# Norms of the first batch and weight magnitudes moved into the last unit of the first attention

## The chip, the cores and the metric

The kernel runs on one core of one Trainium2 chip. The metric is the device time of one execution in microseconds (us). The core has five engines that work side by side, each through its own queue and in its own order: TensorE (PE in the profile, with its weight loads as PEld), VectorE (DVE), ScalarE (ACT), GpSimd (POOL) and SyncE (SP, which issues DMAs). They wait for one another by semaphores.

## The reference, cut to what matters

Four layers follow one another on x, of shape (2, 1024, 256): an attention with 16 heads, a feed-forward with ternary weights, a small attention with 32 heads, and a gated feed-forward. The change touches the seam between the first two.

```python
x = x + layernorm(attention_0(layernorm(x)))
x = x + layernorm(ffn_0(layernorm(x)))
...
def ffn_0(x):                       # w1, w2: (704, 256), w3: (256, 704)
    q = lambda w: clip(round(w / (mean(abs(w)) + 1e-8)), -1, 1)
    return (sigmoid(x @ q(w1).T) * (x @ q(w2).T)) @ q(w3).T
```

So between attention_0 and ffn_0 there are two layer norms (of the attention's result y, and then of the new x) and three sums of |w|, one for each weight.

## The kernel before, in words

x and y live on chip as 16 tiles of 128 tokens by 256 features; tiles 0 to 7 are the first batch, 8 to 15 the second.

`attention_0` runs 32 units u = 2h + b, one for each of the 16 heads h and the two batches b. A unit has eight steps p, one for each tile of queries, in the order of sizes 8, 1, 7, 2, 6, 3, 5, 4 blocks of 128 keys. For each step there is a chain: PE scores, DVE maximum (L801), ACT exponent (L673), PE transposes (L524), ACT high half (`turned_hi`, L668), DVE low half (`turned_lo`, L796), PE context (L539). The engines' orders are written out by hand in `unit`: at step p PE turns step p+1 and scores step p+3, ACT copies the turned step p+1 and takes the exponent of p+3, DVE makes the low half of p+1 and the maximum of p+3. After step 3 and step 7 ACT and DVE split the context (L679, L805), and PE multiplies it by the output weights (`out`, L504), whose result DVE adds to y (`add_out`, L787). The last two add_out of a unit are done at p = 1 of the next unit. So y of the first batch is final after the add_out calls at p = 1 of the last unit (u = 31, a unit of the second batch), and y of the second batch is final with the last instructions of the attention. In the last unit nothing of a next unit is to be projected, and POOL (which rotates queries and keys) has nothing left to do.

Then comes a barrier of all engines (`end_phase`) and `normed_ffn`. Its ramp: ACT sums the magnitudes of the three weights (L949, one Abs over 1536 columns each), DVE takes statistics of y's tiles (L142), the variance (L152 to L157), ACT the square root (L163), DVE the normaliser (L169 to L175); ACT scales four tiles of y and POOL adds them to x (L1241); then POOL scales (L1252) and adds the others. The same norm steps follow for x's first four tiles, ACT scales these (`scale_x`, L1101), PE turns them (L1044), ACT and DVE split them (L1108, L1181). The first half of the ternary weights is made on DVE by `weights.vector(0)` (L959 to L968) after a small matmul of the totals (L954), the second half by `weights.vector(1)`, the third matrix by `weights.vector(2)`.

The body has 4 chunks of 512 tokens (ch), each with 6 hidden tiles (ht), s = 6 ch + ht. For each s: PE `gate_up` (L1057, 8 matmuls of 512 columns), ACT `sigmoid` (L1114), DVE `product` (L1196), ACT `hidden_high` (L1121), DVE `hidden_low` (L1201). PE may begin s only when product s-2 is done. At ht = 0 the variance of the next chunk's x, at ht = 1 its normaliser and scale_x, at ht = 4 of chunk 0 its turning; `down` (L1072) of a chunk runs at ht = 1 of the next. The square root, the exponential and the sigmoid need different tables on ACT, so each change between them is an ACT_TABLE_LOAD in the trace. Copy, Identity and Abs run with any of these tables.

Of the kernel before, what the change touches and what calls it, by code (L numbers as in the profile page):

```python
# [124 lines left out]
class Moments:  # L125
# [22 lines left out]
    def variance(self, dve, g):  # L148
        t0, t1 = self.groups[g]
        dve.wait_ge(self.stats_ready, t1)  # L150
# [120 lines left out]
def program(nc, ins, out):  # L271
    with ExitStack() as ctx:
        c = Core(nc, ctx)
        constants(c, ins["L0_attn_hidden_states"])
        with ExitStack() as wctx:
            raw = RawWeights(c, "f0", F0, [ins[f"L0_ffn_w{j}"] for j in (1, 2, 3)], wctx)
            attention_0(c, ins, lambda loads: norm_and_turn(c, "in", LoadPadded(c, raw, loads)), raw)
            c.end_phase()
            normed_ffn(c, "f0", Ternary(c, raw, wctx), WSCALE, 1.0, True)
# [19 lines left out]
def attention_0(c, ins, before, raw):  # L299
# [22 lines left out]
    with ExitStack() as ctx:  # L322
# [87 lines left out]
        with nc.Block() as block:  # L410
# [28 lines left out]
            def _(pool):  # L439
# [197 lines left out]
            def _(act):  # L637
# [43 lines left out]
                def unit(h, b):  # L681
                    u = 2 * h + b
                    for p in range(TB):
# [33 lines left out]
                        if p == 7 and exists(u + 2):  # L717
                            rope_hi(u + 2, b, 0)

# [29 lines left out]
                units(act, unit)  # L749

            @block.vector
            def _(dve):
# [56 lines left out]
                def unit(h, b):  # L809
                    u = 2 * h + b  # L810
                    for p in range(TB):
# [35 lines left out]
                        if p == 7:  # L847
                            add_out(u, h, b, 1)

# [22 lines left out]
                add_out(NU - 1, H0 - 1, 1, 3)  # L872

# [54 lines left out]

class Ternary:
# [4 lines left out]
    def __init__(self, c, raw, ctx):  # L934
        self.c, self.raw = c, raw
        self.total = c.psum[:, 4, 0:3]
        self.scrap = c.sb("scrap", [P, raw.cols], F32, ctx)
        self.mag, self.gam, self.pos, self.neg = (c.sb(f"q_{n}", [P, 3], F32, ctx) for n in ("mag", "gam", "pos", "neg"))
# [3 lines left out]
        self.mag_ready, self.total_ready, self.thr, self.below_ready, self.ready = (  # L942
            c.sem(n) for n in ("mag_ready", "total_ready", "thr", "below_ready", "q_ready"))

    def scalar(self, act, j):
        if j == 0:
            act.wait_ge(self.raw.loaded, self.raw.landed)
        wait(act, self.mag_ready, j)
        act.activation(self.scrap[:, :], self.raw.buf[:, j, :], ACT.Abs,  # L949
                       accum_out=self.mag[:, j:j + 1]).then_inc(self.mag_ready, 1)  # L950

    def tensor(self, pe):
        pe.wait_ge(self.mag_ready, 3)
# [45 lines left out]
def normed_ffn(c, name, weights, y_unit, unscale, sigmoid_only, out=None):  # L999
# [12 lines left out]
    by_chunk = [(TPC * ch, TPC * ch + TPC) for ch in range(CHUNKS)]  # L1012

    with ExitStack() as ctx:
# [6 lines left out]
        y_norm = Moments(c, f"{name}_y", [(0, NT // 2), (NT // 2, NT)], ctx, y_unit)  # L1021
        x_norm = Moments(c, f"{name}_x", by_chunk, ctx)
# [12 lines left out]
        with c.nc.Block() as block:  # L1035
# [54 lines left out]
            def _(act):  # L1090
# [6 lines left out]
                def scale_x(ch):  # L1097
                    act.wait_ge(x_norm.norm_ready, 2 * ch + 2)
                    wait(act, turned, 2 * (ch - 1))
                    for t in range(TPC * ch, TPC * ch + TPC):  # L1100
                        act.activation(xn[:, ch % 2, t % TPC:t % TPC + 1, :], c.x[:, t:t + 1, :], ACT.Identity,  # L1101
                                       bias=x_norm.shift[:, t:t + 1], scale=x_norm.rstd[:, t:t + 1]).then_inc(xn_ready, 1)
# [20 lines left out]
                def result(ch):  # L1123
                    act.wait_ge(x_added, TPC * ch + TPC)
# [11 lines left out]
                x_norm.root(act, 0)  # L1136
                scale_x(0)
                y_norm.root(act, 1)
                high(0)
                for ch in range(CHUNKS):  # L1140
                    for ht in range(HT):
                        s = ch * HT + ht
                        sigmoid(s)
                        if s >= 1:
                            hidden_high(s - 1)
                        if ht == 0 and ch + 1 < CHUNKS:
                            x_norm.root(act, ch + 1)
# [18 lines left out]
            def _(dve):  # L1166
                def x_variance(ch):
                    dve.wait_ge(x_added, TPC * ch + TPC)
                    x_norm.statistics(dve, c.x, TPC * ch, TPC * ch + TPC)
                    x_norm.variance(dve, ch)  # L1170
# [33 lines left out]
                y_norm.statistics(dve, c.y, 0, NT // 2)  # L1204
                y_norm.variance(dve, 0)
                y_norm.normaliser(dve, 0)
                y_norm.statistics(dve, c.y, NT // 2, NT)
                x_variance(0)
                x_norm.normaliser(dve, 0)
                y_norm.variance(dve, 1)  # L1210
                weights.vector(dve, 0)
                low(0)
                y_norm.normaliser(dve, 1)
                weights.vector(dve, 1)
                for ch in range(CHUNKS):
                    for ht in range(HT):
                        s = ch * HT + ht
                        product(s)
                        if s >= 1:
                            hidden_low(s - 1)  # L1220
                        if ht == 0 and ch + 1 < CHUNKS:
                            x_variance(ch + 1)
                        if ht == 1 and ch + 1 < CHUNKS:
                            x_norm.normaliser(dve, ch + 1)
# [14 lines left out]
            def _(pool):  # L1239
# [6 lines left out]
                for t in range(TPC):  # L1246
                    pool.wait_ge(y_normed, t + 1)
                    add_y(t)
                for t in range(TPC, NT):
                    if t == NT // 2:  # L1250
                        pool.wait_ge(y_norm.norm_ready, 4)
                    pool.tensor_scalar(c.y[:, t:t + 1, :], c.y[:, t:t + 1, :], y_norm.rstd[:, t:t + 1], y_norm.shift[:, t:t + 1],  # L1252
                                       ALU.mult, ALU.add).then_inc(y_scaled, 1)
                    pool.wait_ge(y_scaled, t - TPC + 1)
# [578 lines left out]
```

## Time and profile before

| | us |
|---|---|
| median of 3 runs | 1802.39 (1800.43 to 1804.83) |
| the profiled execution, whole time | 1805.49 |
| its span, first to last instruction | 1803.7 |
| first attention, up to the barrier | about 937.6 |
| ramp of the first feed-forward, to its first gate matmul | 937.6 to 957.2 |
| its chunk 0, to the first matmul of chunk 1 | 957.2 to 981.1 |

Over the span PE is busy 90%, DVE 76%, ACT 61%, POOL 38%; the mean granted TensorE clock is 0.961. These shares are averages over all four layers. The slices around the middle of the span (each 45 us) show PE falling from 9 tenths to 5 and 6 at the seam, with DVE still at 7 and 8. The profiled execution is 3.1 us longer than the median.

The rows further down come from two views. In the busy time by stretch, a row gives the stretch (us from the start of the span), its length, the busy us and number of instructions of PE, PEld, DVE, ACT and POOL, the granted TensorE clock (1.00 is the full 2.4 GHz, 0.50 is 1.2 GHz), and the DMA share and GB/s. In the timeline, a row gives start, duration, engine, line, operation, output <- inputs, shapes, count, and in brackets the idle time before it and what ended it.

### The profile page before, as it was taken

What the parts mean: (1) busy time and instruction counts of PE and PEld (TensorE: products, weight loads), DVE (VectorE), ACT (ScalarE), POOL (GpSimd) and SP (SyncE); (2) the same over time, 40 slices, a digit from 0 to 9 for tenths busy, and PEclk for the clock granted to TensorE, in tenths of its full rate; (3) what the DMA queues carried; (4) which work ended last, traced back from release to release, by engine and by line L of the source; (5) the groups of instructions that cost most, each with busy time, mean ns of one, the idle gap of its engine ahead of it and who ended that gap; (6) DMA issues with size and microseconds to landing.
All of it is one profiled execution on the core that took longest, in us unless ns stands there. A gap on an engine that the chain in (4) does not pass through costs nothing. (4 is left out here: it accounts for less than half of the span.)

```text
span 1803.7 us, 42731 instructions
## 1 busy us (share of the span) xinstructions
PE 1622.6 (90%) x14612; PEld 1012.8 (56%) x14612; DVE 1364.0 (76%) x2792; ACT 1091.7 (61%) x2092; POOL 691.3 (38%) x804
## 2 busy tenths in 40 slices
PE   3899999999999999999956838899999999985997
PEld 1577777777777777777743534233333333333555
DVE  3477877877887887887767657988888888936674
ACT  4566666666666666666645652356566666665553
POOL 1655555555555555555503235021212222224012
PEclk9899999999999999999987969999999999987999
DMA  4322111121121121121100030000000010000001
GB/s 137 93 51 49 46 43 47 44 55 44 44 47 44 44 55 44 44 53 38 35 1 0 1 109 12 16 16 13 17 13 17 12 18 11 10 1 1 1 13 36
DMA packets 53108, 61.85 MB, mean 34 GB/s; under 512 B 11345, under 2 KB 32018, under 8 KB 53010
## 3 DMA queue, kind: packets, MB, share of 16 engines
q1 hardware_dynamic: 53010, 60.55, 13.8%
q8 instruction: 61, 1.00, 0.2%
q14 instruction: 37, 0.30, 0.1%
HBM read 18.57 MB, written 2.10 MB: 11 GB/s over the span
## 5 line engine op out<-in xcount | busy, mean ns | idle before, releaser
L1634 ACT ACTIVATE a_prob<-psum 128x1024 f32<-128x1024 f32 (+3 forms) x384 | 290.8, 812 | 188.8 <-PE psum L1598 188.8
L1674 DVE TENSOR_REDUCE a_mx<-psum 128x1 f32<-128x512 f32 (+3 forms) x608 | 369.2, 656 | 41.3 <-PE psum L1580 28.3
L1666 POOL TENSOR_SCALAR_AFFINE_SELECT a_prob<-a_prob 128x256 f32<-128x256 f32 x256 | 103.0, 408 | 386.8 <-ACT a_prob L1634 384.2
L1577 PE MATMUL psum<-a_kd,a_qp 128*128 128x512 f16 (+3 forms) x768 | 223.0, 337 | 17.8 <-DVE a_mx L1674 6.8
L445 POOL TENSOR_TENSOR a_swp<-a_swp,a_sin 128x512 f32<-128x512 f32 x128 | 163.4, 1276 | 161.6 <-DMA a_swp<-a_lin 130.8
L801 DVE TENSOR_REDUCE a_nmax<-psum 128x1 f32<-128x1024 f32 (+7 forms) x256 | 191.3, 748 | 0.6 <-PE psum L516 0.6
L673 ACT ACTIVATE a_prob_big<-psum,a_nmax 128x1024 f32<-128x1024 f32 (+3 forms) x128 | 122.0, 953 | 102.9 <-DVE a_nmax L801 101.2
L1577 PEld LDWEIGHTS psum<-a_kd,a_qp 128*128 128x128 f16 x768 | 70.6, 98 | 188.1 <-DVE a_mx L1674 139.0
L449 POOL TENSOR_TENSOR a_rope<-a_swp,a_cosd 128x512 f32<-128x512 f32 x128 | 164.2, 1282 | 12.5 <-POOL a_swp L445 4.8
L1619 PE MATMUL psum<-a_prob,a_vg 128*32 128x512 f32 (+3 forms) x1536 | 164.5, 500 | 1.9 <-POOL a_prob L1666 1.4
L796 DVE TENSOR_TENSOR a_pt_lo_big<-psum,a_pt_hi_big 128x512 f16<-128x512 f32 (+3 forms) x256 | 138.5, 582 | 30.2 <-ACT a_pt_hi_big L668 30.2
L539 PE MATMUL psum<-a_pt_hi_big,a_v_hi 128*128 128x128 f16 x832 | 146.0, 219 | 1.3 <-issue 1.0
L539 PE MATMUL psum<-a_pt_hi_big,a_v_lo 128*128 128x128 f16 x832 | 146.0, 219 | 0.0
L539 PE MATMUL psum<-a_pt_lo_big,a_v_hi 128*128 128x128 f16 x832 | 145.9, 219 | 0.0
L455 POOL TENSOR_TENSOR a_q_lo<-a_rope,a_q_hi 128x512 f16<-128x512 f32 x64 | 78.3, 1225 | 141.4 <-ACT a_q_hi L650 141.4
L771 DVE SCALAR_TENSOR_TENSOR a_cosd<-psum,a_head_bias,a_cos 128x512 f32<-128x512 f32 x128 | 95.8, 749 | 40.7 <-ACT a_lin L643 34.6
L643 ACT ACTIVATE a_lin<-psum,a_head_bias 128x512 f32<-128x512 f32 x128 | 88.7, 693 | 61.6 <-PE psum L482 59.9
L515 PE MATMUL psum<-a_k_hi,a_q_hi 128*128 128x512 f16 (+3 forms) x384 | 125.7, 327 | 0.0
L515 PE MATMUL psum<-a_k_lo,a_q_hi 128*128 128x512 f16 (+3 forms) x384 | 125.3, 326 | 0.0
L515 PE MATMUL psum<-a_k_hi,a_q_lo 128*128 128x512 f16 (+3 forms) x384 | 123.7, 326 | 0.0
L524 PE MATMUL psum<-ident,a_prob_big 128*128 128x128 f32 x832 | 116.4, 276 | 4.8 <-ACT y L745 3.5
L668 ACT ACTIVATE a_pt_hi_big<-psum 128x512 f16<-128x512 f32 (+3 forms) x256 | 118.5, 522 | 1.6 <-PE psum L524 1.5
(278 smaller groups left out, 4391.6 us busy)
## 6 DMA issues: line engine op xcount, KB each, us to landing
a_swp<-a_lin SPq DMA_DIRECT2D x256, 128.0 KB, 2.3
a_qp<-a_q_part SPq DMA_DIRECT2D x192, 16.0 KB
a_kd<-a_k_part SPq DMA_DIRECT2D x192, 16.0 KB
x<-_attn_hidden_states_dram SPq DMA_DIRECT2D x4, 512.0 KB, 5.6
a_w_raw<-in_L_attn_Wq_dram SPq DMA_DIRECT2D x16, 128.0 KB, 2.3
a_w_raw<-in_L_attn_Wk_dram SPq DMA_DIRECT2D x16, 128.0 KB, 2.3
a_w_raw<-in_L_attn_Wv_dram SPq DMA_DIRECT2D x16, 128.0 KB, 2.3
a_wo_raw<-in_L_attn_Wo_dram SPq DMA_DIRECT2D x1, 2048.0 KB
```

What stands on the lines that cost most here:

```text
L445: pool.tensor_tensor(swp[:, ch, :], swp[:, ch, :], sin[:, (i % 2) * BANK:(i % 2 + 1) * BANK], ALU.mult).then_inc(sin_done, 1)
L449: pool.tensor_tensor(rope[:, ch, :], swp[:, ch, :], cosd[:, ch, :], ALU.add).then_inc(rope_ready, 1)
L515: last = pe.matmul(scores(p, a, e), qq[:, b, rows], kk[:, b, a:e], start=(m == 0), stop=(m == 2 and e < n))
L539: last = pe.matmul(dst, vv[:, b, j, :], pp[p % 2][:, (p // 2) % 2, cols], start=(j == 0 and m == 0), stop=(j == BLOCKS[p] - 1 and m == 2))
L668: act.activation(pt_hi[p % 2][:, (p // 2) % 2, j0 * P:j1 * P], c.psum[:, turned_bank(at), 0:(j1 - j0) * P], ACT.Copy).then_inc(pt_hi_done, 1)
L673: act.activation(prob[p % 2][:, (p // 2) % 2, 0:BLOCKS[p] * P], scores_row(p), ACT.Exp, bias=nmax[:, b, p:p + 1], accum_out=rowsum[:, b, p ...
L796: dve.tensor_tensor(pt_lo[p % 2][:, (p // 2) % 2, cols], c.psum[:, turned_bank(at), 0:(j1 - j0) * P], pt_hi[p % 2][:, (p // 2) % 2, cols], ...
L801: dve.tensor_reduce(nmax[:, b, p:p + 1], scores_row(p), AX.X, ALU.max, negate=True).then_inc(max_done, 1)
L1577: last = pe.matmul(to[:, j * n:(j + 1) * n], qp[:, w % 3, t * P:(t + 1) * P], kd[:, w % 3, j0 + j, a:e], start=True, stop=not edge)
L1619: last = pe.matmul(c.psum[j * R:(j + 1) * R, 4, a % BANK:a % BANK + e - a], vg[:, u % 2, kt, :], prob_at(u, 2 * n)[:, j, a % BANK:a % BANK ...
L1634: act.activation(prob_at(u, i)[:, 2 * pair:2 * pair + 2, a % BANK:a % BANK + e - a], c.psum[:, pair_of(u, i):pair_of(u, i) + 2, 0:e - a], ...
L1674: dve.tensor_reduce(mx[:, t, j0:j0 + per, a // BANK], work(("S", w, i))[:, 0:per * (e - a)].rearrange("p (j n) -> p j n", j=per), AX.X, AL ...
```

## The change

The norm of y's first batch, its addition to x, the norm of x's first four tiles and the three magnitudes are issued inside the last unit of the attention by a new helper `FirstBatch`; what is left of the norms of the second batch goes into chunk 0 of the feed-forward.

```diff
 (attention_0: GpSimd, after its loop)
+                lead.gpsimd(pool)
 (attention_0: ACT, at the end of each step p of a unit)
+                        if not exists(u + 1):
+                            lead.scalar(act, p, wo_raw[:, 0:raw.cols // D, :].rearrange("p h d -> p (h d)"))
 (ACT, after the units)
+                lead.scalar_last(act)
 (attention_0: DVE, at the end of each step p)
+                        if not exists(u + 1):
+                            if p == 1:
+                                dve.wait_ge(y_done, 4 * u)
+                            lead.vector(dve, p)
 (DVE, after the last add_out)
+                lead.vector_last(dve)
...
+class FirstBatch:
+    def vector(self, dve, p):
+        if p == 1:
+            self.y_norm.statistics(dve, self.c.y, 0, TB)
+            self.y_norm.variance(dve, 0)
+        if p == 3:
+            self.y_norm.normaliser(dve, 0)
+    def vector_last(self, dve):
+        dve.wait_ge(self.x_added, TPC)
+        self.x_norm.statistics(dve, self.c.x, 0, TPC)
+        self.x_norm.variance(dve, 0)
+        self.x_norm.normaliser(dve, 0)
+    def scalar(self, act, p, scrap):
+        if p == 2:
+            self.y_norm.root(act, 0)
+        if p in (4, 5, 6):
+            j = p - 4
+            if j == 0:
+                act.wait_ge(self.raw.loaded, self.raw.landed)
+            wait(act, self.mag_ready, j)
+            act.activation(scrap, self.raw.buf[:, j, :], ACT.Abs, accum_out=self.mag[:, j:j + 1]).then_inc(self.mag_ready, 1)
+    def scalar_last(self, act):
+        self.x_norm.root(act, 0)
+        act.wait_ge(self.mag_ready, 3)
+    def gpsimd(self, pool):
+        y, x = self.c.y, self.c.x
+        pool.wait_ge(self.y_norm.norm_ready, 2)
+        for t in range(TB):
+            pool.tensor_scalar(y[:, t:t + 1, :], y[:, t:t + 1, :], self.y_norm.rstd[:, t:t + 1], self.y_norm.shift[:, t:t + 1],
+                               ALU.mult, ALU.add).then_inc(self.y_scaled, 1)
+            pool.wait_ge(self.y_scaled, t + 1)
+            pool.tensor_tensor(x[:, t:t + 1, :], x[:, t:t + 1, :], y[:, t:t + 1, :], ALU.add).then_inc(self.x_added, 1)
+        pool.wait_ge(self.x_added, TB)
...
 (Ternary: no Abs any more, and PE's wait for the magnitudes goes)
     def tensor(self, pe):
-        pe.wait_ge(self.mag_ready, 3)
...
 (normed_ffn: ACT)
                 weights.scalar(act, 0)
-                y_norm.root(act, 0)
-                scale_y()
+                if not lead:
+                    y_norm.root(act, 0)
+                    scale_y()
...
+                        if lead and ch == 0 and ht == 2:
+                            y_norm.root(act, 0)
 (normed_ffn: DVE)
+                if lead:
+                    weights.vector(dve, 0)
+                    low(0)
+                else:
...
                 weights.vector(dve, 1)
                 for ch in range(CHUNKS):
                     for ht in range(HT):
                         s = ch * HT + ht
                         product(s)
                         if s >= 1:
                             hidden_low(s - 1)
+                        if lead and ch == 0 and ht == 1:
+                            y_norm.statistics(dve, c.y, NT // 2, NT)
+                            y_norm.variance(dve, 0)
+                        if lead and ch == 0 and ht == 3:
+                            y_norm.normaliser(dve, 0)
```

In the first feed-forward `y_norm` now covers the second batch alone and `x_norm` chunks 1 to 3, and POOL begins with tile 8. The Abs results that nobody reads go into the raw output weights, which are no longer needed, in place of a buffer of their own. The second feed-forward is built without the helper and is as before.

## Rows read from the trace of the kernel before

**Rows 1.** Busy time by stretch: last unit, ramp, chunk 0.
```profile
907.00:937.60 30.60, 21.54 (x227) 17.38 (x227) 19.03 (x42) 11.92 (x29) 0.00 (x0) 0.93 0.00 1
937.60:957.16 19.56, 2.69 (x10) 1.93 (x10) 17.18 (x60) 13.04 (x21) 7.92 (x12) 0.50 0.00 1
957.16:981.10 23.94, 17.38 (x56) 6.79 (x57) 18.52 (x40) 11.88 (x20) 12.22 (x16) 0.71 0.00 1
```

**Rows 2.** Timeline, last unit: start, duration, engine, line, [idle before, releaser].
```profile
918.78 0.58 ACT L673 ACTIVATE a_prob_small<-psum,a_nmax 128x384 f32<-128x384 f32 x1 [1.10 <-DVE a_nmax L801]
...
919.35 0.86 ACT L668 ACTIVATE a_pt_hi_big<-psum 128x512 f16<-128x512 f32 x2
...
921.76 0.79 ACT L673 ACTIVATE a_prob_big<-psum,a_nmax 128x640 f32<-128x640 f32 x1 [0.79 <-DVE a_nmax L801]
...
923.06 0.56 DVE L796 TENSOR_TENSOR a_pt_lo_small<-psum,a_pt_hi_small 128x384 f16<-128x384 f32 x1 [0.65 <-ACT a_pt_hi_small L668]
...
924.93 0.76 ACT L668 ACTIVATE a_pt_hi_big<-psum 128x512 f16<-128x512 f32 x2
...
927.05 0.60 ACT L668 ACTIVATE a_pt_hi_small<-psum 128x512 f16<-128x512 f32 x1 [1.37 <-PE psum L524]
...
930.75 0.60 ACT L679 ACTIVATE a_ctx_hi<-psum 128x512 f16<-128x512 f32 x1 [3.10 <-PE psum L539]
...
935.23 0.88 DVE L787 SCALAR_TENSOR_TENSOR y<-psum,a_rsum,y 128x256 f32<-128x256 f32 x2 [0.41 <-PE psum L504]
```

**Rows 3.** Timeline, the ramp of the first feed-forward.
```profile
937.64 1.48 ACT L949 ACTIVATE scrap<-f_raw 128x1536 f32<-128x1536 f32 x1 [6.29 <-PEq L81]
937.66 2.71 DVE L142 BATCH_NORM_STATS2 f_y_stats<-y 128x6 f32<-128x256 f32 x8 [1.56 <-PEq L81]
...
939.23 1.28 ACT L163 ACT_TABLE_LOAD   x1
...
941.25 0.21 ACT L163 ACTIVATE f_y_sd<-f_y_var 128x8 f32<-128x8 f32 x1 [0.74 <-DVE f_y_var L157]
941.57 0.20 DVE L169 RECIPROCAL f_y_inv<-f_y_sd 128x8 f32<-128x8 f32 x1 [0.35 <-ACT f_y_sd L163]
...
942.56 0.16 DVE L175 TENSOR_SCALAR f_y_rstd<-f_y_half 128x8 f32<-128x8 f32 x1
...
947.96 0.59 PE L954 MATMUL psum<-q_mag,ones 128*128 128x3 f32 x2 [12.77 <-ACT scrap L949]
...
951.06 2.08 ACT L1101 ACTIVATE f_xn<-x,f_x_shift,f_x_rstd 128x256 f32<-128x256 f32 x4 [1.34 <-DVE f_x_rstd L175]
...
952.65 0.62 DVE L965 TENSOR_SCALAR below<-f_raw,q_neg 128x768 f16<-128x768 f32 x1
...
957.17 0.61 PE L1057 MATMUL psum<-xT_hi,ternary 128*128 128x512 f16 x1 [2.86 <-DVE xT_lo L1181]
```

**Rows 4.** Timeline, chunk 0.
```profile
959.82 1.08 DVE L965 TENSOR_SCALAR below<-f_raw,q_neg 128x768 f16<-128x768 f32 x1
...
962.05 0.68 DVE L1196 TENSOR_TENSOR f_hid<-psum,f_sig 128x512 f32<-128x512 f32 x1
...
967.23 0.60 ACT L1114 ACTIVATE f_sig<-psum 128x512 f32<-128x512 f32 x1
...
968.69 0.58 PE L1057 MATMUL psum<-xT_hi,ternary 128*128 128x512 f16 x1 [4.00 <-DVE f_hid L1196]
...
973.54 0.58 ACT L1114 ACTIVATE f_sig<-psum 128x512 f32<-128x512 f32 x1
...
978.57 0.68 DVE L1196 TENSOR_TENSOR f_hid<-psum,f_sig 128x512 f32<-128x512 f32 x1
...
981.10 0.39 PE L1057 MATMUL psum<-xT_hi,ternary 128*128 128x512 f16 x1 [0.73 <-DVE xT_lo L1181]
```

**Rows 5.** Stretches of the L1057 matmuls alone: s = 3, and s = 6.
```profile
968.60:973.00 4.40, 3.57 (x8) 1.02 (x8) 0.50 0.00 0
981.05:982.80 1.75, 1.70 (x8) 0.79 (x9) 1.00 0.00 0
```

More of the change, by code:

```diff
@@ L296, in spans, with attention_0 @@
         lo = end
-def attention_0(c, ins, before, raw):
+def attention_0(c, ins, before, raw, lead):
     nc = c.nc
@@ L926, in gpsimd_first, with __init__ @@
             pool.memset(buf[:, :, raw.width:raw.tiles * P] if j < 2 else buf[:, raw.width // P, :], 0.0).then_inc(self.padded, 1)
+class FirstBatch:
+    TILES = TB
+    def __init__(self, c, raw, ctx):
+        self.c, self.raw = c, raw
+        self.y_norm = Moments(c, "lead_y", [(0, TB)], ctx, WSCALE)
+        self.x_norm = Moments(c, "lead_x", [(0, TPC)], ctx)
+        self.mag = c.sb("q_mag", [P, 3], F32, ctx)
+        self.y_scaled, self.x_added, self.mag_ready = (c.sem(n) for n in ("lead_y_scaled", "lead_x_added", "lead_mag_ready"))
+    def vector(self, dve, p):
[30 more added lines that the diff above has]
+        pool.wait_ge(self.x_added, TB)
@@ L941, in __init__, with scalar @@
         self.parts = [[raw.view(self.ternary, j)] for j in range(3)]
[L942 to L950, printed above, removed]
+        self.total_ready, self.thr, self.below_ready, self.ready = (
+            c.sem(n) for n in ("total_ready", "thr", "below_ready", "q_ready"))
+    def scalar(self, act, piece):
+        pass
     def tensor(self, pe):
-        pe.wait_ge(self.mag_ready, 3)
         pe.matmul(self.total, self.c.ones[:, :], self.mag[:, :], start=True, stop=True).then_inc(self.total_ready, 1)
@@ L996, in vector, with normed_ffn @@
                                      in1=self.parts[j][0][:, :, cols], op0=ALU.mult, op1=ALU.subtract).then_inc(self.ready, 1)
-def normed_ffn(c, name, weights, y_unit, unscale, sigmoid_only, out=None):
+def normed_ffn(c, name, weights, y_unit, unscale, sigmoid_only, out=None, lead=None):
     HT = weights.raw.tiles
@@ L1101, in scale_x @@
                         act.activation(xn[:, ch % 2, t % TPC:t % TPC + 1, :], c.x[:, t:t + 1, :], ACT.Identity,
-                                       bias=x_norm.shift[:, t:t + 1], scale=x_norm.rstd[:, t:t + 1]).then_inc(xn_ready, 1)
+                                       bias=norm.shift[:, t:t + 1], scale=norm.rstd[:, t:t + 1]).then_inc(xn_ready, 1)
                 def high(ch):
@@ L1123, in result @@
                 def result(ch):
-                    act.wait_ge(x_added, TPC * ch + TPC)
+                    wait(act, x_added, TPC * ch + TPC - DONE)
                     for i in range(2):
@@ L1167, in x_variance @@
                 def x_variance(ch):
-                    dve.wait_ge(x_added, TPC * ch + TPC)
+                    wait(dve, x_added, TPC * ch + TPC - DONE)
                     x_norm.statistics(dve, c.x, TPC * ch, TPC * ch + TPC)
-                    x_norm.variance(dve, ch)
+                    x_norm.variance(dve, ch - X0)
                 def e_variance(ch):
@@ L1202, in hidden_low @@
                                       ALU.subtract).then_inc(hid_lo, 1)
[L1204 to L1213, printed above, removed]
+                if lead:
+                    weights.vector(dve, 0)
+                    low(0)
+                else:
+                    y_norm.statistics(dve, c.y, 0, NT // 2)
+                    y_norm.variance(dve, 0)
+                    y_norm.normaliser(dve, 0)
+                    y_norm.statistics(dve, c.y, NT // 2, NT)
+                    x_variance(0)
+                    x_norm.normaliser(dve, 0)
+                    y_norm.variance(dve, 1)
+                    weights.vector(dve, 0)
+                    low(0)
+                    y_norm.normaliser(dve, 1)
                 weights.vector(dve, 1)
@@ L1220, in _ @@
                             hidden_low(s - 1)
+                        if lead and ch == 0 and ht == 1:
+                            y_norm.statistics(dve, c.y, NT // 2, NT)
+                            y_norm.variance(dve, 0)
+                        if lead and ch == 0 and ht == 3:
+                            y_norm.normaliser(dve, 0)
                         if ht == 0 and ch + 1 < CHUNKS:
```

48 lines of the change are left out of this document (28 added, 20 removed).

## The prediction

> **What bounds the kernel at the seam.** I read the busy time by stretch first, then the timeline of each engine from 907 to 990 us, then the waits. The stretches [rows 1] show three pieces. The ramp, from the barrier to the first gate matmul, is 19.56 us with PE busy for 2.69 of them: this is the time the change is after. The last unit of the attention is not full either: in 30.6 us PE is busy 21.54, DVE 19.03, ACT 11.92 and POOL 0. It looks as if there were room for everything. The timeline says otherwise [rows 2]. Each exponent waits for DVE's maximum (idle 1.10 and 0.79), each low half on DVE waits for ACT's high half (0.65), and the high half at 919.35 and the one at 924.93 start right behind an exponent with no idle at all. So in this unit ACT and DVE take turns on one chain: maximum, exponent, turning, high half, low half, the next maximum. Their idle time is the other's turn. What is put into either queue on its turn lengthens the chain one for one; what is put where that engine waits anyway is free up to the length of that wait.
>
> **What goes into the last unit, in order of steps p.**
> - p = 1, DVE: eight statistics and the variance, from 937.66 to the root at 941.25 [rows 3], so 3.6 us, ahead of the maximum for which the exponent at 918.78 waits. On the chain: +3.6.
> - p = 2, ACT: the root, a table load of 1.28 and a root of 0.21 with gaps [rows 3], between the exponent at 918.78 and the high half at 919.35, which had no idle before it [rows 2]: +1.6.
> - The exponent table has to be loaded again before the exponent at 921.76. That one idles 0.79 [rows 2], and the 1.28 fits but for 0.5; ACT gets there a little earlier after the root, since PE will have caught up: bounds 0.3 and 0.5, taken +0.4.
> - p = 3, DVE: the normaliser, 941.57 to 942.72, 1.15 [rows 3]. DVE idles 0.65 there, plus the 0.4 just gained: +0.1.
> - p = 4, ACT: the first Abs, 1.6 from its start at 937.64 to the next start at 939.23 [rows 3], ahead of the high half at 924.93 that had no idle [rows 2]: +1.6.
> - p = 5, ACT: the second Abs, ahead of the high half at 927.05 that idles 1.37 [rows 2]: +0.2.
> - p = 6, ACT: the third, ahead of the context copy that idles 3.10 [rows 2]: 0.
> - POOL's eight tiles begin after the normaliser; at 12.22 us for 16 instructions [rows 1] a tile (two instructions) is 1.5 us, four are ready 6 us later, all eight 12 us later, and the unit has some 15 us to go. Covered. The new wait on y_done at p = 1 is for DVE's own previous instructions: nothing.
>
> Sum of the last unit: 3.6 + 1.6 + 0.4 + 0.1 + 1.6 + 0.2 = +7.5.
>
> **Behind the last add_out** (935.23 plus 0.88 [rows 2]) DVE alone does x's norm: half of the eight statistics, 1.35, then variance, root and normaliser as in rows 3; 942.72 - 937.66 - 1.35 = 3.7. The square root's table load hides in ACT's wait. The barrier follows at the same distance as before. +3.7.
>
> **The ramp.** Once y's norm, x's norm and the magnitudes are gone, two chains start with the block. ACT's scale_x at 951.06 led to the gate matmul at 957.17, 6.1 us [rows 3]; that is the upper end, since half of it was a wait for DVE. DVE's thresholds: the matmul of the totals, 0.59, three small operations of 0.16 with their waits, about 0.5, then 957.17 - 952.65 = 4.5 [rows 3]. Together 5.65, taken. The ramp was 957.17 - 937.64 = 19.5, so -13.9. PE's removed wait costs nothing on its own, it is in this sum.
>
> **Chunk 0, counted from its first gate matmul.** Before, product 0 came at 4.9, held by the second half of the ternary weights on a DVE that POOL was slowing (the same operation takes 0.62 at 952.65 and 1.08 at 959.82 [rows 3, 4], POOL working beside the second). Now POOL is idle there and PE's eight matmuls at the lower clock, 3.5 us [rows 5], come last: -1.35. From product 0 to sigmoid 1 it was 5.2 (962.05 to 967.23 [rows 4]), now product 0.6, statistics and variance 2.2, root and table load 1.55: -0.8. So sigmoid 1 is 2.15 earlier. Then DVE takes the second batch's eight statistics and variance ahead of the normaliser that scale_x(1) and sigmoid 2, behind it on ACT, wait for: +3.55, less 0.3 for the now undisturbed normaliser; balance +1.1. At ht = 2 ACT loads the root's table, takes the root and loads the sigmoid's again ahead of the sigmoid that stood at 973.54: 2.9 by rows 3; DVE had 0.4 us of its own there, so the chain is at +3.6. At ht = 3 DVE has the normaliser, +1.15, and then the third weight matrix beside POOL, which has just been released: by the 0.62 and 1.08 above, between 0 and +1.4 for its first operation and little for its second, taken +0.9. The product at 978.57 and with it the low half that PE waits for at 981.10 [rows 4] come 5.7 later relative to the first gate.
>
> **The clock.** PE idled 4.00 us before 968.69, and the following eight matmuls took 3.57 us at a granted clock of 0.50 (1.2 GHz); at 981.10 it had idled 0.73 and they took 1.70 at 1.00 (2.4 GHz) [rows 4, 5]. With chunk 0 stretched, PE will idle some 5 us before chunk 1, and its first eight matmuls stand on the path: +1.8. In the last unit PE will idle about 4 us before the last turning; the context and output matmuls behind it are on the path. Bounds 0 (clock stays) and +2.6 (all that follows at half); taken +1.2.
>
> **The sum.** 7.5 + 3.7 - 13.9 + 5.7 + 1.8 + 1.2 = +6.0 us. From chunk 1 on nothing is changed but POOL's tiles, which end before the next norm, so the shift is carried to the end. On its own execution 1805.5 becomes 1811.5; on the median 1802.4 becomes 1808.4.
>
> **A rule against the change.** In the trace a table load costs 1.28 us and the next activation starts at once (939.23; in the ramp it even runs ahead of the wait for the variance [rows 3]).
> The Trainium skill, ScalarE: Activation LUTs, What ACT_TABLE_LOAD costs, adds a drain of about 1.38 us to every switch. By that rule four added switches on the path would cost 5.5 us more and the time would be 1813.9; the trace does not show such a drain, so it has a small chance here.
>
> **The rivals.**
> - The idle shares are real room: what is inserted in the last unit hides. Then only the tail, ramp and chunk 0 count: 3.7 - 13.9 + 5.7 + 1.8 = -2.7, no measurable change; and if the second batch's statistics, root and normaliser in chunk 0 hide as well (-5.7 - 1.8), -10.2, that is 1792.2. For it: PE runs up to three steps ahead. Against: the four brackets in rows 2 and the high halves that start without idle. It turns faster once more than 9.6 of the 15 us on both chains hide. Chance 0.13, spread from 1792 to 1798.
> - The steps are as told but the clock does not fall in either place and the contention is nil: 6.0 - 1.8 - 1.2 - 0.9 = +2.1, 1804.5, within the noise. Chance 0.3 for this and for a partial hiding.
> - The clock falls in the last unit and stays low through the tail: +2.6 in place of 1.2, with the full 1.4 of contention: +7.9, 1810.3. Chance 0.14. With the drain on top, 1813.9 or more: 0.03.
> - POOL's additions come late and DVE waits for x_added ahead of the barrier. The cover is 9 us (four tiles ready 6 us after the normaliser, 15 to go); only if a tile took 3.7 us, against 1.5, would it show. 0.02, and +1 or +2.
>
> **How the numbers follow.** The forecast as summed, between 1806 and 1810, has 0.38. A measurement of this kernel can tell about 0.2%, 3.6 us, from no change: faster means under 1798.8, slower over 1806.0. From the cases: faster 0.13, same 0.30, slower 0.57. The range leaves out most of the fast case and the drain: 1800.5 to 1812.5.
>
> **What would show it.** In the profile of the changed kernel: the barrier about 11 to 13 us later than 937.6; gate 0 5.6 us after it, about 954 to 956; the exponent of step 5 waiting for the maximum behind the statistics; two more table loads in the last unit and two more in chunk 0; sigmoid 3 preceded by one; the first matmul of chunk 1 between 984 and 987 at a clock of 0.50 after an idle of 4 us or more. The forecast is wrong if the barrier comes less than 8 us later (room in the last unit), or if the first matmul of chunk 1 comes before 981 (room in chunk 0).

## The result, and the profile after

The changed kernel takes 1808.57 us (median of 20 runs, 1803.78 to 1810.96) against 1802.05 (median of 20, 1800.43 to 1804.83). The ratio of the runs is 1.0031, 95% interval 1.0024 to 1.0037: slower by 5.6 us (4.3 to 6.7). The forecast was 1808.4, +6.0. The profiled execution took 1808.71, its span is 1807.0.

The busy time by stretch of the kernel after: last unit with its tail and the barrier, ramp, chunk 0. Columns as in [rows 1].

```profile
905.00:947.90 42.90, 25.81 (x227) 20.16 (x227) 26.27 (x78) 20.47 (x40) 10.14 (x16) 0.79 0.00 1
947.90:953.50 5.60, 2.66 (x10) 1.93 (x10) 4.82 (x10) 4.55 (x7) 0.00 (x0) 0.50 0.00 0
953.50:982.20 28.70, 15.75 (x56) 6.27 (x56) 20.04 (x54) 14.55 (x23) 5.08 (x4) 0.74 0.00 1
```

The ramp went from 19.56 to 5.6 us, as meant. The last unit and chunk 0 grew by more than that: 30.6 to 42.9 (with the tail in it) and 23.9 to 28.7.

The last unit in the timeline of the kernel after, DVE and ACT, with PE's last turning; it answers to [rows 2]. L675 is the exponent, L670 the high half, L973 the Abs.

```profile
914.34 1.65 DVE L792 SCALAR_TENSOR_TENSOR y<-psum,a_rsum,y 128x256 f32<-128x256 f32 x4
916.03 2.71 DVE L142 BATCH_NORM_STATS2 lead_y_stats<-y 128x6 f32<-128x256 f32 x8
...
920.41 0.58 ACT L675 ACTIVATE a_prob_small<-psum,a_nmax 128x384 f32<-128x384 f32 x1 [4.68 <-DVE a_nmax L806]
...
921.10 1.28 ACT L163 ACT_TABLE_LOAD   x1
...
922.51 0.85 ACT L670 ACTIVATE a_pt_hi_big<-psum 128x512 f16<-128x512 f32 x2
...
923.87 1.28 ACT L675 ACT_TABLE_LOAD   x1
925.16 0.79 ACT L675 ACTIVATE a_prob_big<-psum,a_nmax 128x640 f32<-128x640 f32 x1
...
928.33 1.47 ACT L973 ACTIVATE a_wo_raw<-f_raw 128x1536 f32<-128x1536 f32 x1
...
929.80 0.75 ACT L670 ACTIVATE a_pt_hi_big<-psum 128x512 f16<-128x512 f32 x2
...
931.25 1.09 PE L526 MATMUL psum<-ident,a_prob_small 128*128 128x128 f32 x4 [3.35 <-DVE a_pt_lo_big L801]
...
932.38 0.60 ACT L670 ACTIVATE a_pt_hi_small<-psum 128x512 f16<-128x512 f32 x1 [0.36 <-PE psum L526]
...
937.44 0.60 ACT L681 ACTIVATE a_ctx_hi<-psum 128x512 f16<-128x512 f32 x1 [3.00 <-PE psum L541]
...
941.90 0.88 DVE L792 SCALAR_TENSOR_TENSOR y<-psum,a_rsum,y 128x256 f32<-128x256 f32 x2 [0.41 <-PE psum L506]
```

Ahead of the statistics nothing was changed, and the group of four add_out operations in front of them is the point from which both traces are counted (916.30 in the kernel before, 914.34 here; in the fourteen profiles of this study it lies between 912.95 and 916.30, so the first 900 us alone differ by up to 3 us from one execution to another, and spans are compared less well than steps). What to see: the exponent of step 5 waits 4.68 us where it waited 1.10, then come a table load, the root, another table load, and at 928.33 an Abs where the high half used to stand. The last turning takes 1.09 in place of 0.63.

The ramp and chunk 0 of the kernel after, answering to [rows 3, 4]:

```profile
942.69 1.40 DVE L142 BATCH_NORM_STATS2 lead_x_stats<-x 128x6 f32<-128x256 f32 x4
...
953.52 0.61 PE L1114 MATMUL psum<-xT_hi,ternary 128*128 128x512 f16 x1 [2.35 <-DVE xT_lo L1245]
...
963.43 2.70 DVE L142 BATCH_NORM_STATS2 f_y_stats<-y 128x6 f32<-128x256 f32 x8
...
971.08 1.28 ACT L163 ACT_TABLE_LOAD   x1
972.37 0.21 ACT L163 ACTIVATE f_y_sd<-f_y_var 128x8 f32<-128x8 f32 x1
972.60 1.28 ACT L1173 ACT_TABLE_LOAD   x1
973.89 0.60 ACT L1173 ACTIVATE f_sig<-psum 128x512 f32<-128x512 f32 x1
...
977.80 2.00 DVE L1023 SCALAR_TENSOR_TENSOR ternary<-f_raw,q_pos,below 128x1536 f16<-128x1536 f32 x1
...
978.28 2.10 POOL L1314 TENSOR_TENSOR x<-x,y 128x256 f32<-128x256 f32 x1
...
982.25 0.61 PE L1114 MATMUL psum<-xT_hi,ternary 128*128 128x512 f16 x1 [4.93 <-DVE xT_lo L1245]
...
985.94 0.69 DVE L1260 TENSOR_TENSOR f_hid<-psum,f_sig 128x512 f32<-128x512 f32 x1 [2.55 <-PE psum L1114]
...
989.14 0.71 DVE L155 TENSOR_SCALAR f_x_m<-f_x_m 128x4 f32<-128x4 f32 x1
```

The same five marks read in every profiled execution of the study, in us. Unit: from the four add_out operations at step 1 of the last unit to the end of the last add_out. Seam: from there to the first gate matmul. Chunk 0: from there to product 6 (the first of chunk 1). Variance: product 6 to product 7. The sum is that of the four. These columns are read from one execution of each kernel, and the ratio from all its runs. The profiled executions of e5, e10 and e12 took 1803.73, 1795.62 and 1803.24 us, 4 to 5 us less than the medians of their kernels, that of e4 took 4 us more (1808.06): so the sums and the ratios need not agree, and steps say more than sums.

| kernel | unit | seam | chunk 0 | variance | sum | ratio of the runs to before (95%) |
|---|---|---|---|---|---|---|
| before | 19.8 | 21.1 | 25.9 | 5.6 | 72.4 | |
| after | 28.4 | 10.7 | 32.4 | 6.6 | 78.2 | 1.0031 (1.0024 to 1.0037) |
| e1_stats_early | 22.1 | 21.0 | 26.5 | 5.6 | 75.2 | 1.0018 (1.0010 to 1.0027) |
| e2_stats_late | 19.9 | 21.0 | 25.9 | 5.6 | 72.4 | 1.0003 (0.9994 to 1.0011) |
| e3_clock_fill | 26.8 | 10.7 | 30.9 | 6.5 | 74.9 | 1.0016 (1.0007 to 1.0025) |
| e4_root_joined | 27.9 | 10.7 | 29.0 | 6.1 | 73.8 | 1.0003 (0.9994 to 1.0012) |
| e5_mag_late | 24.8 | 10.8 | 30.4 | 7.0 | 72.8 | 1.0020 (1.0009 to 1.0031) |
| e6_norm_late | 19.7 | 13.7 | 32.3 | 6.7 | 72.5 | 0.9995 (0.9986 to 1.0003) |
| e7_both | 20.3 | 13.2 | 27.9 | 5.9 | 67.4 | 0.9977 (0.9968 to 0.9987) |
| e8_early_second | 20.3 | 13.5 | 27.5 | 5.8 | 67.0 | 0.9971 (0.9960 to 0.9982) |
| e9_unit_fill | 26.9 | 10.7 | 32.4 | 6.6 | 76.7 | 1.0016 (1.0007 to 1.0024) |
| e10_both_fill | 20.2 | 13.2 | 27.9 | 5.9 | 67.3 | 0.9982 (0.9973 to 0.9990) |
| e11_early_fill | 20.0 | 13.5 | 25.9 | 5.9 | 65.3 | 0.9960 (0.9947 to 0.9973) |
| e12_pool_hold | 27.9 | 10.7 | 30.4 | 5.9 | 75.0 | 1.0032 (1.0019 to 1.0044) |

### The profile page after: what moved, and what is told of

It reads as the page before. It is cut to its first block and busy times, and to the rows that moved or that the text cites. A ratio compares the mean times of both kernels' runs of the same rounds, so it can differ in the third digit from the quotient of the medians.

```text
span 1807.0 us, 42735 instructions
## 1 busy us (share of the span) xinstructions
PE 1626.9 (90%) x14612; PEld 1015.5 (56%) x14612; DVE 1360.6 (75%) x2792; ACT 1094.4 (61%) x2092; POOL 694.3 (38%) x808
## 5 line engine op out<-in xcount | busy, mean ns | idle before, releaser
L675 ACT ACTIVATE a_prob_big<-psum,a_nmax 128x1024 f32<-128x1024 f32 (+3 forms) x128 | 122.0, 953 | 102.5 <-DVE a_nmax L806 100.7
L456 POOL TENSOR_TENSOR a_q_lo<-a_rope,a_q_hi 128x512 f16<-128x512 f32 x64 | 78.2, 1221 | 140.6 <-ACT a_q_hi L652 140.6
L526 PE MATMUL psum<-ident,a_prob_big 128*128 128x128 f32 x832 | 116.9, 276 | 8.2 <-DVE a_pt_lo_small L801 4.2
L670 ACT ACTIVATE a_pt_hi_big<-psum 128x512 f16<-128x512 f32 (+3 forms) x256 | 118.5, 522 | 1.6 <-PE psum L526 1.5
```

Of the source, the lines that this page charges most:

```text
L670: act.activation(pt_hi[p % 2][:, (p // 2) % 2, j0 * P:j1 * P], c.psum[:, turned_bank(at), 0:(j1 - j0) * P], ACT.Copy).then_inc(pt_hi_done, 1)
L675: act.activation(prob[p % 2][:, (p // 2) % 2, 0:BLOCKS[p] * P], scores_row(p), ACT.Exp, bias=nmax[:, b, p:p + 1], accum_out=rowsum[:, b, p ...
```

## The experiments

**Is the last unit one chain, or has it room?** Eight statistics that nobody reads are put into the kernel before, once at step 1, once split over steps 4 and 5.

```diff
+                        if not exists(u + 1) and p == 1:          # e1_stats_early
+                            dve.wait_ge(y_done, 4 * u)
+                            for t in range(TB):
+                                dve.bn_stats(extra[:, t, :], c.y[:, t:t + 1, :])
...
+                        if not exists(u + 1) and p in (4, 5):     # e2_stats_late
+                            for t in range(4 * (p - 4), 4 * (p - 3)):
+                                dve.bn_stats(extra[:, t, :], c.y[:, t:t + 1, :])
```

> The kernel before, with eight more statistics of y's finished first batch on DVE at the end of step 1 of the last unit; nobody reads them. One-chain theory (ACT and DVE take turns, no slack at that point): the last unit and the whole kernel get 2.7 us longer, 1804.7 against 1802.1, and up to 1.5 more if TensorE's clock falls in the longer gaps. Rival (the idle shares of the last unit are room): 0 to +0.5 us.

> The kernel before, with the same eight statistics, but four at the end of step 4 and four at the end of step 5, where DVE waits 1.33 and 1.24 us for ACT. One-chain theory: they hide in these waits but for 0.1 to 0.3 us, so the time of before. A theory by which any added DVE work costs its duration: +2.7. The rival (room everywhere) gives 0 here too; only together with the run before do the two theories part.

Measured: 1806.33 and 1803.43 against 1802.86, so +3.2 us (1.8 to 4.9) and +0.5 (-1.1 to 2.0). The unit grew by 2.3 and by 0.1 us. In the timeline of e1, the exponent behind the statistics, and in that of e2 the high half of step 6 and the low half behind it:

```profile
916.59 2.71 DVE L853 BATCH_NORM_STATS2 a_extra<-y 128x6 f32<-128x256 f32 x8
...
920.12 0.58 ACT L674 ACTIVATE a_prob_small<-psum,a_nmax 128x384 f32<-128x384 f32 x1 [3.83 <-DVE a_nmax L802]
```

```profile
922.21 1.39 DVE L852 BATCH_NORM_STATS2 a_extra<-y 128x6 f32<-128x256 f32 x4
...
923.01 0.75 ACT L669 ACTIVATE a_pt_hi_big<-psum 128x512 f16<-128x512 f32 x2
923.63 0.89 DVE L797 TENSOR_TENSOR a_pt_lo_big<-psum,a_pt_hi_big 128x512 f16<-128x512 f32 x2
```

In e1 ACT waits for the statistics (3.83 for 1.10 [rows 2]). In e2 they end just as the high half is there, and the low half starts without idle where it had waited 1.33. The same work, 2.7 us, costs 2.3 in one place and nothing in another. The theory of one chain stands; that the idle shares are room is wrong for step 1 and right for steps 4 and 5.

**Does the clock stand on the path?** In the changed kernel PE gets matmuls whose result nobody reads: 18 behind hidden tile 5 of chunk 0 (e3), or 12 in step 5 of the last unit (e9).

```diff
+                        if lead and ch == 0 and ht == HT - 1:     # e3_clock_fill, PE
+                            for n in range(18):
+                                pe.matmul(c.psum[:, 5, :], w_parts[0][0][:, 0, 0:P], c.xT_hi[:, 0, 0:BANK], start=True, stop=True)
...
+                        if p == 5 and not exists(u + 1):          # e9_unit_fill, PE
+                            for n in range(12):
+                                pe.matmul(c.psum[:, 0, :], w_hi[:, 0, 0, :], c.xT_hi[:, 0, 0:BANK], start=True, stop=True)
```

> The changed kernel, with 18 matmuls of 512 columns whose result nobody reads, on PE behind hidden tile 5 of chunk 0, where it idles 4.9 us before chunk 1. If the clock's fall is what makes the first eight matmuls of chunk 1 slow (and the runs differ by whether it falls), they run at the upper clock: 1.7 us less, 1806.8 against 1808.5, and a smaller spread. Rival (the slow matmuls are not on the path): no difference.

> The changed kernel, with 12 matmuls of 512 columns whose result nobody reads, on PE in step 5 of the last unit, ahead of its 3.35 us wait for the last turning. The prediction put 1.2 us on the clock's fall there (bounds 0 and 2.6). If that is so: about 1807.3 against 1808.5, the last turning and the context behind it at the upper clock. Rival (the slow matmuls behind the gap are hidden): 1808.5. The interval of such a run is about 1.5 us wide on either side, so the timeline decides.

Measured: e3 1805.97 (ratio 1.0016, where the changed kernel has 1.0031), e9 1806.05 (1.0016). PE in e3, then PE in e9:

```profile
977.47 4.05 PE L1149 MATMUL psum<-xT_hi,ternary 128*128 128x512 f16 x18
981.36 0.38 PE L1117 MATMUL psum<-xT_hi,ternary 128*128 128x512 f16 x1
```

```profile
927.98 2.75 PE L609 MATMUL psum<-xT_hi,a_w_hi 128*128 128x512 f16 x12
930.57 0.60 PE L526 MATMUL psum<-ident,a_prob_small 128*128 128x128 f32 x4
```

With its gap filled, chunk 1's first matmul takes 0.38 in place of 0.61, and chunk 0 with product 6 is 1.6 us shorter. The three profiles with a gap of 4.6 to 5.0 us there and no fill (changed kernel, e6, e9) all have the slow matmuls, so e3's timeline and its ratio say the same: they were on the path.

In the last unit the timeline of e9 alone would not show it. From the start of the last turning to the end of the unit it takes 9.7 us, as in the kernel before, in place of the changed kernel's 11.5; but the same stretch, without a fill, is 10.9 in e12, 11.0 in e4, and 9.9 in e3, whose last turning is as slow as the changed kernel's:

```profile
931.85 1.09 PE L526 MATMUL psum<-ident,a_prob_small 128*128 128x128 f32 x4 [2.15 <-DVE a_pt_lo_big L801]
```

How far the clock falls there differs from one execution to another (granted clock over this stretch 0.65 in the changed kernel, 0.69 in e4 and e12, 0.83 in e3, 0.87 in e9 and before). What speaks for e9 is its ratio, 0.0015 below that of the changed kernel. For both e3 and e9 this is 2.7 us, give or take 2 (an estimate from the two intervals): more than nothing, but not by much, and in keeping with the 1.7 and 1.2 that were expected. Added work on PE made the kernel faster in both places, so the slow matmuls were on the path. e3 was to have a smaller spread too; 5.2 us over 12 runs against 7.2 over 20 does not show it.

Of the changed kernel's 20 runs the four below 1806 us have a mean granted clock of 0.965 to 0.967, the thirteen above 1808 one of 0.959 to 0.962. The seam is only one of the places where they part. The kernel before goes from 1799.80 to 1806.98 in the 35 runs beside e1 to e4, as wide a spread. Between the profiled executions of the changed kernel (span 1807.0, clock 0.959) and of e12 (1801.5, 0.967), 1.0 us of the difference lies ahead of the last unit's mark, 3.2 in the four stretches (0.7 of them e12's edit) and 1.3 behind; the granted clock is 0.76 against 0.85 from 950 to 1000 us, but also 0.83 against 0.89 from 1650 to 1700. Over all profiles the part behind product 7, nearly the same work in each, takes 812.4 to 816.7 us.

**Chunk 0: the second batch's norm in better places.** Its root stands beside x's root and its normaliser where DVE waits.

```diff
 (ACT)
-                        if lead and ch == 0 and ht == 2:
+                        if lead and ch == 0 and ht == 0:          # behind x_norm.root
                             y_norm.root(act, 0)
 (DVE: statistics and variance behind x_variance at ht == 0, normaliser behind x's at ht == 1)
```

> The changed kernel, with the second batch's statistics and variance at hidden tile 0 of chunk 0 instead of 1, its root beside x's root there (one stay of the root's table instead of two), and its normaliser behind x's at tile 1, where DVE then waits for ACT. Chain theory: 2.95 us of table loads and 1.15 of normaliser leave the path, so 4.1 less; PE's idle before chunk 1 shrinks below what made the clock fall, 1.7 less; POOL's tiles end before the variance in chunk 1, 1.0 less: 4 to 7 us less, 1802 to 1804.5. If ACT's table loads are hidden there: no difference.

Measured: 1804.03, ratio 1.0003, 4.5 to 5 us less than the changed kernel. Chunk 0 is 3.4 shorter, 2.85 of it ahead of chunk 1's first matmul: 4.1 were expected. Counted from the first gate matmul, sigmoid 3 came 2.9 sooner, as the table loads say, but product 3 only 2.0: POOL, released earlier, now works beside DVE there, and two of DVE's hidden_low take 1.16 and 1.05 in place of 0.68.

```profile
972.09 1.16 DVE L1265 TENSOR_TENSOR f_hidT<-f_hid,f_hidT 128x512 f16<-128x512 f32 x1
...
980.31 0.39 PE L1114 MATMUL psum<-xT_hi,ternary 128*128 128x512 f16 x1 [3.57 <-DVE xT_lo L1245]
```

PE's gap is 3.57, and the first product of chunk 1 follows after 3.1 us, neither 2.0 (clock kept) nor 3.7: the first two matmuls take 0.39 and 0.38, from the fourth on they take 0.63.

**The magnitudes, then the first norm, in the last unit.**

```diff
 (e5_mag_late, ACT)
-        if p in (4, 5, 6):
-            j = p - 4
...
...
+    def scalar_last(self, act, scrap):
+        act.wait_ge(self.raw.loaded, self.raw.landed)
+        for j in range(3):
+            wait(act, self.mag_ready, j)
+            act.activation(scrap, self.raw.buf[:, j, :], ACT.Abs, accum_out=self.mag[:, j:j + 1]).then_inc(self.mag_ready, 1)
 (e6_norm_late, also)
+        if p in (4, 5):
+            self.y_norm.statistics(dve, self.c.y, 4 * (p - 4), 4 * (p - 3))
+        if p == 6:                                                # and the root on ACT at p == 6
+            self.y_norm.variance(dve, 0)
+            self.y_norm.normaliser(dve, 0)
```

> The changed kernel, with all three magnitudes on ACT behind the context copy of step 7 in the last unit, where ACT waits 5.6 us for the variance of x. Chain theory: the first Abs (1.5 us, ahead of a high half that had no idle) and the rest of the second leave the path: 1.8 to 2.3 us less than the changed kernel, about 1806.4. Rival (ACT's idle share is room): no difference, 1808.5.

> As the run before, and y's first norm moved as well: four statistics on DVE at the end of step 4, four at step 5, variance, root and normaliser at step 6, all where its engine waits for another; the root comes behind the last exponent, so that the exponent's table is not loaded again. POOL then ends its fourth tile about 1 us behind the last add_out. Chain theory: the last unit costs 0.5 in place of 8.6 us, the tail 0.7 more: 7 to 8 less than the changed kernel, 1800.5 to 1801.5. If the place did not matter: 1808.5.

Measured: e5 1807.81 (ratio 1.0020), e6 1801.50 (0.9995). e5 is unclear by its time alone: 0.8 us less by the medians, 2 by the ratios, with intervals that overlap. The timeline of e5 settles what the Abs cost:

```profile
926.91 0.69 ACT L675 ACTIVATE a_prob_small<-psum,a_nmax 128x512 f32<-128x512 f32 x1 [1.23 <-DVE a_nmax L806]
...
929.91 0.60 ACT L670 ACTIVATE a_pt_hi_small<-psum 128x512 f16<-128x512 f32 x1 [1.37 <-PE psum L526]
```

From the exponent of step 7 to the last high half it is 3.0 us, in the changed kernel 4.7 (927.65 to 932.38), before the change 2.8: 1.7 us. Of these 1.3 lie ahead of the last turning and are the first Abs; 0.5 are the turning itself, 0.63 in e5 and 1.09 in the changed kernel. The second Abs cost nothing: the high half at 932.38 waits for the turning [0.36 <-PE psum L526]. The rest of e5's unit is 2 us shorter as well, at a granted clock of 1.00 from the last turning on; its profiled execution is among the five shorter of its twelve runs (1800.68 to 1804.33), the seven others took 1807.69 to 1809.27.

e6 takes the unit back to 19.7, that of the kernel before, with the whole first norm in it. But its seam is 3.0 us longer than that of the changed kernel, where 0.7 was expected:

```profile
934.17 1.41 DVE L142 BATCH_NORM_STATS2 lead_x_stats<-x 128x6 f32<-128x256 f32 x4 [0.96 <-POOL x L984]
...
936.96 0.42 DVE L157 SCALAR_TENSOR_TENSOR lead_x_var<-lead_x_sq,lead_x_m 128x4 f32<-128x4 f32 x1
...
938.79 0.72 POOL L984 TENSOR_TENSOR x<-x,y 128x256 f32<-128x256 f32 x1
...
941.34 1.09 ACT L1158 ACTIVATE f_xn<-x,lead_x_shift,lead_x_rstd 128x256 f32<-128x256 f32 x2 [3.73 <-PEq L81]
```

DVE waits 0.96 for POOL's fourth tile. Three of its small operations take 0.42 to 0.64 in place of 0.16 while POOL does the other four tiles, 1.0 us in all. And POOL ends its eighth at 939.51, 0.6 behind DVE's last operation, so that the barrier, which waits for it, comes 0.8 later. These three make the 3.0. The prediction's rival of late additions by POOL, which did not come true in the changed kernel, does here.

**Together, and further.**

> The run before together with the joined root in chunk 0, which by itself gave 4.5 us. The two stretches do not overlap, so they add: 1796 to 1797.5, faster than both kernels. If the clock takes back a part at each gap: 1798 to 1799.

> The run before, with six of the second batch's eight statistics inside the attention: three at step 7, where DVE waits 1.0 us for PE, three behind the last add_out, where it waits for POOL's fourth tile. They leave the chain of chunk 0, 0.34 us each: 1.5 to 2.0 less, about 1795. If the waits were not there: as the run before, since the same work only changes its place.

> The late norm and the joined root together (1798.0 median), with PE kept busy in chunk 0 in its two longest gaps: 15 such matmuls behind hidden tile 2, 9 behind tile 5. If the clock's fall at the 5.7 us gap is on the path there: 1 to 2 us less, 1796 to 1797, and the runs closer together. Rival (behind that gap the path goes over DVE and ACT, PE's slow matmuls have slack): 1798.

> The kernel with the late norm, the joined root and six of the second batch's statistics in the attention (1798.4), which did not gain the 2 us that left chunk 0; its trace has PE 3.6 us idle before chunk 1 and slow matmuls behind it. Now with 12 matmuls whose result nobody reads in that gap. If the clock took the gain back: chunk 1's first product comes 1.5 us sooner after its first matmul (2.0 in place of 3.5), and the time is 1796.5 to 1797. If the gain was lost elsewhere: 1798.4.

```diff
 (e8_early_second, DVE; the feed-forward then takes statistics of two tiles only)
+                            if p == 7:
+                                dve.wait_ge(y_done, 4 * u + 2)
+                                lead.second(dve, (7, 0, 6))
...
+                dve.wait_ge(y_done, 4 * NU)
+                lead.second(dve, (1, 5, 2))
...
 (e10_both_fill: e7 with 15 such matmuls at ht == 2 and 9 at ht == 5; e11_early_fill: e8 with these 12, PE)
+                        if lead and ch == 0 and ht == HT - 1:
+                            for n in range(12):
+                                pe.matmul(c.psum[:, 5, :], w_parts[0][0][:, 0, 0:P], c.xT_hi[:, 0, 0:BANK], start=True, stop=True)
```

Measured: e7 1798.00 (0.9977), e8 1798.42 (0.9971), e10 1799.52 (0.9982), e11 1794.81 (0.9960, six runs; the kernel before, run beside it, 1803.27). e7 is 3.5 us below e6, where the joined root alone had given 4.5 to 5: the two edits' sum within the intervals, though half a us above the 1796 to 1797.5 expected. e8 was to gain 1.5 to 2.0 more; its median gained nothing, its ratio 1.1 us, within the intervals. Chunk 0 up to chunk 1's first matmul did get 2.0 shorter (25.9 to 23.9), and then this, e8 first, e11 second:

```profile
972.05 0.45 PE L1127 MATMUL psum<-xT_hi,ternary 128*128 128x512 f16 x1 [3.57 <-DVE xT_lo L1258]
...
975.58 0.69 DVE L1273 TENSOR_TENSOR f_hid<-psum,f_sig 128x512 f32<-128x512 f32 x1 [2.39 <-PE psum L1127]
```

```profile
967.02 2.75 PE L1162 MATMUL psum<-xT_hi,ternary 128*128 128x512 f16 x12
...
970.74 0.39 PE L1130 MATMUL psum<-xT_hi,ternary 128*128 128x512 f16 x1 [0.97 <-DVE xT_lo L1264]
...
972.73 0.69 DVE L1279 TENSOR_TENSOR f_hid<-psum,f_sig 128x512 f32<-128x512 f32 x1 [0.85 <-PE psum L1130]
```

In e8 the product comes 3.5 us after the first matmul, at a granted clock of 0.53, in e11 2.0, at 1.00. So in this execution of e8 the clock took 1.5 of the 2.0 back. That the fill returned them is not shown by this pair: two profiles with the same gap and no fill (e5, e12) have 2.0 as well, and the ratio of e11, 2.0 us below that of e8, is within the intervals. In e10 the fill behind tile 2 did nothing: its four stretches are those of e7, whose clock had stayed up before chunk 1 anyhow; behind the gap at tile 3 the path goes over DVE and ACT. Its median of 1799.52 speaks for the rival (1798), not for the 1796 to 1797 that were expected if the clock stood on the path there. e11 is faster than both kernels, by 7.2 us (4.9 to 9.6) than the one before.

**Is POOL the cause of the longer variance in chunk 1?**

```diff
 (e12_pool_hold, POOL)
                 for t in range(scaled_first, NT):
+                    if lead and t == 3 * TPC:
+                        pool.wait_ge(x_norm.var_ready, 2)
```

> The changed kernel, with POOL waiting ahead of its last four tiles until the variance of x in chunk 1 is done on DVE. The step from product 6 to product 7 grew by 1.0 us (5.60 to 6.61) and the small operations in it from 0.16 to 0.71 us. If POOL working beside them is the cause: 5.6 again, and the time 1 us less, 1807.5. If not: 6.6.

Measured: the step is 5.9 in place of 6.6, 0.7 of the 1.0; the time, 1808.56, shows nothing, since 0.7 us is far within its interval.

```profile
980.39 0.39 PE L1114 MATMUL psum<-xT_hi,ternary 128*128 128x512 f16 x1 [3.58 <-DVE xT_lo L1245]
...
982.99 1.02 DVE L1265 TENSOR_TENSOR f_hidT<-f_hid,f_hidT 128x512 f16<-128x512 f32 x1
...
985.71 0.17 DVE L155 TENSOR_SCALAR f_x_m<-f_x_m 128x4 f32<-128x4 f32 x1
```

The small operations are back at 0.16 and 0.17, where the changed kernel had 0.37, 0.71 and 0.42. The 0.3 us that remain are the hidden_low at 982.99, 1.02 in place of 0.68, beside POOL's last addition that is not held (982.74 to 983.46). The profiled execution kept the clock up ahead of this step, but so did that of e5, without the hold, and there the step took 7.0: it was not the clock. The step behind it, product 7 to 8, is 6.2 in place of 5.8, so that half of the gain is given back where POOL does its held tiles. So POOL accounts for the whole term, by the timeline alone.

## Why the prediction was right, point by point

It was right in direction, in size and in nearly all its steps; two terms were off by 1 us each, in opposite directions. That they cancelled is in part luck: the second was put at nothing, and its size was worked out nowhere. The +1.2 for the clock in the unit was a middle taken between 0 and 2.6. Shifts in the last unit are counted from the four add_out operations.

| term | predicted | measured |
|---|---|---|
| statistics and variance at step 1 | +3.6 | +3.6 |
| root at step 2 | +1.6 | +1.5 |
| exponent's table again | +0.4 | +0.2 |
| normaliser at step 3 | +0.1 | 0.0 |
| first Abs | +1.6 | +1.5 |
| second Abs (predicted); the turning at the lower clock (measured) | +0.2 | +0.5 |
| rest of the unit at the lower clock | +1.2 | +1.3 |
| tail and ramp | +3.7 - 13.9 = -10.2 | -10.3 |
| chunk 0 to chunk 1's first matmul | +5.7 | +4.8 |
| its first matmuls at the lower clock | +1.8 | +1.7 |
| variance in chunk 1 | 0 | +1.0 |
| sum | +6.0 | +5.8 |

- **The chain in the last unit** was the step on which the sign hung. e1 and e2 show it, and e6 shows the reverse: with the norm in the waits the unit is as short as before. The shares of busy time (ACT 11.92 of 30.6 [rows 1]) had said nothing about it; the brackets with 1.10, 0.79 and 0.65 [rows 2] had.
- **The first mis-sized term** is POOL's contention with the third weight matrix, put at +0.9. It measured +0.2 on DVE (1.82 to 2.00 for the ternary operation, the other one unchanged at 1.01). It was POOL that waited: 1.24 and 2.10 for a scaling and an addition that take 0.56 and 0.72.
- **The second follows from the first.** The prediction said that POOL's tiles end before the next norm. Held up, they ended at 991, behind the variance at 987.2 to 990.4, and DVE paid there: 0.71 for an operation of 0.16. Undisturbed, eight tiles of 1.35 us from 976.95 on would have ended at 987.8, ahead of the small operations (an estimate from the rows of POOL). The contention came in about the forecast total, one stage later.
- **The clock** was rightly put on the path in both places (e3 by timeline and ratio, e9 by its ratio). In this execution it cost 1.8 in the unit, with the turning, against 1.2 forecast, and 1.7 before product 6 against 1.8. It was forecast as if certain, but it differs from one execution to another: the unit's 1.8 is 0.2 in e3, and among the four profiles with a gap of 3.57 to 3.62 us before chunk 1 (e4, e5, e8, e12) the first product came after 3.1, 2.0, 3.5 and 2.0 us. At 4.6, 4.9 and 5.0 it took 3.5, 3.7 and 3.7, at 2.7 (e1) 2.6, at 2.0 and less always 2.0.
- **The rival by the Trainium skill's page ScalarE: Activation LUTs, What ACT_TABLE_LOAD costs** (a drain of about 1.4 us with each switch) falls: at 921.10 and 972.60 in the profile after, the load takes 1.28 and the next activation starts 0.01 us behind it, while the previous one had ended just ahead of the load.
- POOL's additions were covered, as said: its fourth tile was done at 932.1, ten us ahead of the statistics that need it. In e6, where the norm came later, they were not covered.
- Of what was to be seen: the barrier came 12.2 us later (11 to 13 forecast, counted from the same mark), gate 0 5.6 us behind it, chunk 1's first matmul at 982.25 with an idle of 4.93 ahead and at the lower clock. Counted from the mark it would be 984.2 (984 to 987 forecast).

What would have made the change pay: the same work in the waits of the same engines. e7 and e11 do nothing less than the changed kernel and are 10 and 13 us faster than it by their ratios.

## What to carry to other kernels

An engine that is idle 60% of a stage has room only where it waits for the other one at that instruction: before moving work in, read the bracket of the very instruction ahead of which it goes, and take the length of that wait as the room. Where two engines take turns on a chain, an operation that starts without idle has no room ahead of it, however low both shares are. Count the table loads on both sides of a moved square root, and put it behind the last exponential or beside another root. Moved work has followers too: an engine released later may end later than a stage that it must not meet. And where moved work opens a gap of 4.6 us or more on TensorE, expect the matmuls behind it at half speed, as in all three profiles that have one before chunk 1 and no fill; if they start a stage, a few matmuls whose result nobody reads can be worth more than they cost (e3), and where other engines hold the path they give nothing (e10).

## What the runs showed of the hardware

- Filling TensorE's idle time made the kernel faster: 18 matmuls, 4.05 us of pure waste, took 1.7 us off the step from chunk 1's first matmul to its first product in e3 (3.7 to 2.0; granted clock 0.50, 1.2 GHz, behind a gap of 4.9 us without them, 1.00, 2.4 GHz, with them), and 2.7 us off the time by the ratios.
- The fall of the clock behind a gap of about 3.6 us is not a fixed property of the program: four profiles with the same gap differ by 1.5 us behind it. Gaps of 4.6 to 5.0 us at the same place were followed by the lower clock in all three profiles without a fill.
- Beside DVE's ternary operation of 2.00 us POOL's addition took 2.10 us for 0.72, and beside POOL's additions DVE's smallest operations took up to 0.71 for 0.16. In these rows the one that came second paid: the addition began at 978.28 behind DVE's 977.80, the small operation at 989.14 behind POOL's 989.10. A delay of POOL turned into a delay of DVE eight microseconds later.
